# Reordering the opening of a small vision-transformer kernel: TensorE matmuls on constants first, mask coefficients summed on GpSimd

## What is computed

```python
patches = im.reshape(b, c, hp, P, wp, P)                  # P = 8: 256 patches of 2048 numbers per image
x = jnp.einsum('bchpwq,dcpq->bhwd', patches, conv_w)      # 2048 x 128 weights, "conv" below
x = x.reshape(b, hp * wp, -1) + conv_b
for i in range(2):                                        # L = 2 layers, 8 heads of 64
    y = _ln(x, ln1_g[i], ln1_b[i])
    q, k, v = jnp.split(y @ qkv_w[i], 3, axis=-1)
    ...                                                   # softmax(q), softmax(k), ctx = k^T v, att = q ctx
    x = x + att @ out_w[i] + out_b[i]
    x = x + gelu(_ln(x) @ ff1_w[i] + ff1_b[i]) @ ff2_w[i] + ff2_b[i]
h = _ln(x, lnf_g, lnf_b) @ head_w + head_b
h = h + attention3(layernorm(h))
# feed-forward with masks: for e in (96, 144, 192), r in (2, 3, 4): a = alpha_e[e] * alpha_r[r]
C0 = C0 + a * (m_out[:, None] * m_in[None, :])            # m_in = (d < e), m_out = (h < r * e)
h = h + new_gelu(layernorm(h) @ (w_fc * C0).T + b_fc * c0b) @ (w_proj * C1).T + b_proj * c1b
```

## Time and profile before

| | us |
|---|---|
| three timed runs | 151.07, 151.41, 154.46 |
| median of the runs | 151.41 |
| span of the profiled execution (first to last instruction) | 154.1 |
| the run that fits that span, and what it leaves around it | 154.46, 0.4 |
| PE busy / DVE busy / ACT busy / POOL busy within the span | 131.1 / 93.7 / 66.0 / 49.1 |

### The profile page before, as it was taken

The page is one execution under the profiler, slowest core; times in us unless marked ns, Lnnn a source line. Parts: engine busy times, 40 slices in busy tenths (PEclk is TensorE's granted clock), DMA queues, the critical chain, the costliest instruction groups (busy, mean ns, idle before and its releaser), DMA issues.

```text
span 154.1 us, 2173 instructions
## 1 busy us (share of the span) xinstructions
PE 131.1 (85%) x790; PEld 113.1 (73%) x790; DVE 93.7 (61%) x236; ACT 66.0 (43%) x149; POOL 49.1 (32%) x60
## 2 busy tenths in 40 slices
PE   1699889999779989799797996769987959999993
PEld 1468668797658968589576984559876948999992
DVE  1200087947799668977689757773957796145201
ACT  3010313906559746697375981144222040163230
POOL 0000020074162953447553673180671060004000
PEclk9999999999999999999999999956977995599999
DMA  5999997008800000000000000000000000000101
GB/s 161 285 421 415 421 412 262 0 4 265 209 0 0 6 0 0 0 0 4 0 0 0 0 4 0 0 0 2 2 0 0 4 0 0 0 4 0 51 0 51
DMA packets 3388, 11.50 MB, mean 75 GB/s; under 512 B 393, under 2 KB 1385, under 8 KB 3122
## 3 DMA queue, kind: packets, MB, share of 16 engines
q1 hardware_dynamic: 3378, 11.37, 20.6%
HBM read 10.98 MB, written 0.39 MB: 74 GB/s over the span
## 4 chain that ended last, share of the span: by engine, by line
PE 55%; DVE 26%; issue 5%; POOL 5%; ACT 3%; DMA 3%; SPq 0%; DVEq 0%; ACTq 0%; POOLq 0%
PE bank L302 16%; DVE xn L655 10%; PE bank L320 10%; PE bank L437 5%; PE bank L389 5%; PE bank L561 5%; POOL rstd L1103 3%; DMA embed_sb<-in_embed 3%; DVE stats L645 2%; DVE yT_hi L662 2%; DVE nkmax L695 2%; POOL yT_lo L1109 1%; PE bank L336 1%; PE bank L531 1%; PE bank L339 1%
## 5 line engine op out<-in xcount | busy, mean ns | idle before, releaser
L1103 POOL TENSOR_TENSOR rstd<-var,minus_half 128x2 f32<-128x2 f32 x14 | 10.2, 726 | 69.8 <-DVE var L650 69.8
L655 DVE TENSOR_SCALAR xn<-x,mv,rstd 128x128 f32<-128x128 f32 x20 | 13.8, 732 | 4.2 <-POOL rstd L1103 4.2
L320 PE MATMUL bank<-embed_sb 128*128 128x256 f32 x32 | 12.0, 544 | 4.4 <-DMA embed_sb<-in_embed 4.4
L955 ACT ACTIVATE yT<-bank,small_sb 128x256 f32<-128x256 f32 x10 | 5.7, 565 | 19.5 <-DVE yT_hi L662 16.4
L320 PEld LDWEIGHTS bank<-embed_sb 128*128 128x128 f32 x32 | 8.5, 277 | 7.2 <-DMA embed_sb<-in_embed 5.1
L1122 POOL TENSOR_TENSOR qn<-q,rqsum 128x512 f32<-128x512 f32 x8 | 8.2, 1044 | 15.2 <-DVE rqsum L719 15.2
L336 PE MATMUL bank<-small_sb,xn 128*128 128x128 f32 x20 | 4.4, 301 | 7.6 <-DVE xn L655 7.6
L413 PE MATMUL bank<-cw,qT 128*128 128x128 f32 x64 | 10.0, 289 | 0.4
L413 PEld LDWEIGHTS bank<-cw,qT 128*128 128x128 f32 x64 | 8.2, 190 | 2.0 <-issue 1.3
L336 PEld LDWEIGHTS bank<-small_sb,xn 128*128 128x128 f32 x20 | 2.0, 141 | 10.3 <-DVE xn L655 10.3
L975 ACT ACTIVATE kexp<-bank,nkmax 128x256 f32<-128x256 f32 x16 | 7.4, 473 | 4.3 <-DVE nkmax L695 4.3
(11 more groups left out here) (142 smaller groups left out, 349.1 us busy)
## 6 DMA issues: line engine op xcount, KB each, us to landing
embed_sb<-in_embed SPq DMA_DIRECT2D x3, 768.0 KB, 7.9
patches_sb<-in_patches SPq DMA_DIRECT2D x2, 1024.0 KB, 12.1
restw<-in_rest_w SPq DMA_DIRECT2D x2, 768.0 KB, 16.1
qkvw<-in_qkv_w SPq DMA_DIRECT2D x3, 256.0 KB, 11.0
embed_sb<-in_qkv_w SPq DMA_DIRECT2D x1, 768.0 KB, 4.7
embed_sb<-in_embed SPq DMA_DIRECT2D x1, 576.0 KB, 4.4
projw_raw<-in_proj_w SPq DMA_DIRECT2D x1, 576.0 KB, 16.2
embed_sb<-in_fc_w SPq DMA_DIRECT2D x1, 576.0 KB, 7.6
```

The lines of the kernel that those rows point to most:

```text
L320: mm = nc.tensor.matmul(dst[:, 0:TOKENS], embed_sb[:, c, 0:D], rhs, start=(c == 0), stop=(c == KCONV - 1))
L655: last = nc.vector.tensor_scalar(xn[i][:, t, 0:width], src[:, t, 0:width], mv[i][:, t, 0:1], rstd[i][:, t:t + 1], ALU.subtract, ALU.mult)
L1103: nc.gpsimd.tensor_tensor(rstd[i][:], var[i][:], minus_half[:], ALU.pow).then_inc(rstd_ready[i], 1)
```

## The change

1. TensorE's first work is five matmuls of the constant tile `ones` (128x128 by 192 columns) into a bank nobody reads (`warm_up`). They wait only for the first memset of DVE. The first image's 16 chunks then run without the mask matmuls between them.
2. The mask coefficients are no longer made by matmuls. A table of 128 x 9 x 66 numbers (`mix`, 0/1 patterns laid out as the coefficients are used) is loaded with the six alphas, and POOL makes the nine products, weighs the table and adds its nine slices up (`mix_coefficients`, at the end of step 0, behind `ff1w_lo`). DVE's four weighing instructions, PE's nine small matmuls and ACT's three copies are gone.
3. SP's order: the old 9-partition mask load between the second and third piece of the first image is gone; the small constants come one piece later; the second image's patches come in three pieces (chunks 0 to 3, 4 to 7, 8 to 15), the first two where the first half was; the weights of layer 1 come ahead of the projection's; the new table, 297 KB, and the alphas follow them.

```diff
+SECOND_AT = (0, 4, 8, KCONV)
+SECOND_PIECES = len(SECOND_AT) - 1
+WARM_UP = 5
+FC_MIX, PROJ_MIX, BIAS_MIX = 0, ECH * HSEG, ECH * HSEG + HC * (ESEG + 1)
+NMIX = BIAS_MIX + ESEG
...
-        mix_sb = sb("mix_sb", [MIX, HMAX + E + HSEG + ESEG + 2])
+        mix_sb = sb("mix_sb", [P, MIX, NMIX])
+        alphas_sb = sb("alphas_sb", [P, len(EMBED) + len(RATIO)])
...
         @block.sync
         def _(sp):
-            half = KCONV // 2
             for j in range(CONV_PIECES):
                 at = slice(CONV_AT[j], CONV_AT[j + 1])
                 sp.dma_start(embed_sb[:, at, :], embed0[:, at, :]).then_inc(loaded[f"embed{j}"], 16)
-                if j == 1:
-                    sp.dma_start(mix_sb[:], mix).then_inc(loaded["mix"], 16)
+                if j == 2:
                     sp.dma_start(small_sb[:], small).then_inc(loaded["small"], 16)
-            sp.dma_start(patches1_sb[:, 0:half, :], patches1[:, 0:half, :]).then_inc(loaded["patches1a"], 16)
+            def second(j):
+                at = slice(SECOND_AT[j], SECOND_AT[j + 1])
+                sp.dma_start(patches1_sb[:, at, :], patches1[:, at, :]).then_inc(loaded[f"second{j}"], 16)
+            second(0)
+            second(1)
...
-            sp.dma_start(patches1_sb[:, half:, :], patches1[:, half:, :]).then_inc(loaded["patches1b"], 16)
+            second(2)
             sp.dma_start(restw[0][:], rest_w[0]).then_inc(loaded["rest0"], 16)
             sp.dma_start(rows_sb[:], rows.to_broadcast([P, NROW])).then_inc(loaded["rows"], 16)
+            sp.dma_start(restw[1][:], rest_w[1]).then_inc(loaded["rest1"], 16)
+            sp.dma_start(alphas_sb[:], alphas.to_broadcast([P, len(EMBED) + len(RATIO)])).then_inc(loaded["mix"], 16)
+            sp.dma_start(mix_sb[:], mix).then_inc(loaded["mix"], 16)
+            sp.dma_start(headw[:], head_w).then_inc(loaded["head"], 16)
             sp.dma_start(projw_raw[:], proj_w).then_inc(loaded["proj"], 16)
-            sp.dma_start(restw[1][:], rest_w[1]).then_inc(loaded["rest1"], 16)
-            sp.dma_start(headw[:], head_w).then_inc(loaded["head"], 16)
...
+            def warm_up(dst):
+                pe.wait_ge(consts_set, 1)
+                for _ in range(WARM_UP):
+                    nc.tensor.matmul(dst[:, 0:E], ones[:, 0:P], ones[:], start=True, stop=True)
...
-            conv(0, KB[0], 0, CONV_AT[2])
-            mix_fc_masks()
-            conv(0, KB[0], CONV_AT[2], KCONV)
+            warm_up(CB)
+            conv(0, KB[0], 0, KCONV)
             pe.wait_ge(loaded["small"], 16)
             embedding_to_tokens(0, KB[1])
-            pe.wait_ge(mix_copied, 2)
             conv(1, SB_, 0, 6)
...
             head(0)
-            mix_proj_masks()
...
+            def mix_coefficients():
+                pool.wait_ge(loaded["mix"], 32)
+                e, r = alphas_sb[:, 0:len(EMBED)], alphas_sb[:, len(EMBED):]
+                shape = [P, len(EMBED), len(RATIO)]
+                nc.gpsimd.tensor_tensor(alpha[:].rearrange("p (i j) -> p i j", i=len(EMBED)),
+                                        e.unsqueeze(2).to_broadcast(shape), r.unsqueeze(1).to_broadcast(shape),
+                                        ALU.mult).then_inc(mixing, 1)
+                pool.wait_ge(mixing, 1)
+                nc.gpsimd.tensor_tensor(weighted[:], mix_sb[:], alpha[:].unsqueeze(2).to_broadcast([P, MIX, NMIX]),
+                                        ALU.mult).then_inc(mixing, 1)
+                for m in range(1, MIX):
+                    pool.wait_ge(mixing, m + 1)
+                    nc.gpsimd.tensor_tensor(coef[:], weighted[:, 0, :] if m == 1 else coef[:], weighted[:, m, :],
+                                            ALU.add).then_inc(mixing, 1)
+                pool.wait_ge(mixing, MIX + 1)
...
                 if s == 0:
                     weight_low_part("ff1_0", 1, ff1w_all(0), ff1w_parts[0][0][:], ff1w_parts[0][1][:])
+                    mix_coefficients()
```

More of the change, by code:

```diff
@@ L68, with build @@
 CONV_PIECES = len(CONV_AT) - 1
-def build(nc, small, embed0, patches1, qkv_w, rest_w, rows, mix, fc_w, proj_w, head_w, aqkv_w, aout_w, out):
+SECOND_AT = (0, 4, 8, KCONV)
[3 more added lines that the diff above has]
+NMIX = BIAS_MIX + ESEG
+def build(nc, small, embed0, patches1, qkv_w, rest_w, rows, mix, alphas, fc_w, proj_w, head_w, aqkv_w, aout_w, out):
     with ExitStack() as ctx:
@@ L201, in build @@
         loaded = {n: sem(f"loaded_{n}") for n in (
-            ["small", "mix", "rows", "fc", "proj", "head", "aqkv", "aout", "patches1a", "patches1b", "qkv0_k"]
-            + [f"embed{j}" for j in range(CONV_PIECES)]
+            ["small", "mix", "rows", "fc", "proj", "head", "aqkv", "aout", "qkv0_k"]
+            + [f"embed{j}" for j in range(CONV_PIECES)] + [f"second{j}" for j in range(SECOND_PIECES)]
             + [f"qkv{l}" for l in range(LAYERS)] + [f"rest{l}" for l in range(LAYERS)])}
         consts_set = sem("consts_set")
-        alpha_ready = sem("alpha_ready")
-        mix_psum = sem("mix_psum")
-        mix_copied = sem("mix_copied")
+        mixing = sem("mixing")
         split_hi, split_lo = ({n: sem(f"{n}_{part}") for n in ("qkv0", "qkv1", "ff1_0", "ff1_1", "aqkv", "fc")}
@@ L316, in conv @@
                         pe.wait_ge(loaded[f"embed{CONV_AT.index(c)}"], 16)
-                    if i == 1 and c % (KCONV // 2) == 0:
-                        pe.wait_ge(loaded["patches1a" if c == 0 else "patches1b"], 16)
+                    if i == 1 and c in SECOND_AT:
+                        pe.wait_ge(loaded[f"second{SECOND_AT.index(c)}"], 16)
                     rhs = embed_sb[:, c, D:] if i == 0 else patches1_sb[:, c, :]
@@ L439, in ff2 @@
                 mm.then_inc(ff2_done[i], 1)
-            def mix_fc_masks():
-                pe.wait_ge(loaded["mix"], 16)
-                pe.wait_ge(alpha_ready, 3)
-                for c in range(ECH):
-                    nc.tensor.matmul(SB_[0:EC, c * HSEG:(c + 1) * HSEG], alpha_mask_e[:, c * EC:(c + 1) * EC],
-                                     mask_hseg, start=True, stop=True)
-                nc.tensor.matmul(SB_[:, 128:128 + E], alpha[:], mask_e, start=True, stop=True).then_inc(mix_psum, 1)
-            def mix_proj_masks():
-                for c in range(HC):
-                    at = c * (ESEG + 1)
-                    mm = nc.tensor.matmul(KB[1][:, at:at + ESEG + 1], mask_h[:, c * P:(c + 1) * P], alpha_eseg[:],
-                                          start=True, stop=True)
-                mm.then_inc(mix_psum, 1)
+            def warm_up(dst):
+                pe.wait_ge(consts_set, 1)
+                for _ in range(WARM_UP):
+                    nc.tensor.matmul(dst[:, 0:E], ones[:, 0:P], ones[:], start=True, stop=True)
             def head(i):
@@ L1254 @@
     mask_e = np.array([[u < e for u in range(E)] for e in EMBED for r in RATIO], np.float32)
-    alpha_e = np.repeat(a["L0_ffn_alpha_e"], len(RATIO))[:, None]
-    alpha_r = np.tile(a["L0_ffn_alpha_r"], len(EMBED))[:, None]
+    masks = np.zeros((P, MIX, NMIX), np.float32)
+    in_e = mask_e.reshape(MIX, ECH, EC).transpose(2, 0, 1)
+    masks[:EC, :, FC_MIX:PROJ_MIX] = (in_e[:, :, :, None] * mask_h[None, :, None, ::SEG]).reshape(EC, MIX, -1)
+    in_h = mask_h.reshape(MIX, HC, P).transpose(2, 0, 1)
+    seg_e = np.concatenate([mask_e[:, ::SEG], np.ones((MIX, 1), np.float32)], axis=1)
+    masks[:, :, PROJ_MIX:BIAS_MIX] = (in_h[:, :, :, None] * seg_e[None, :, None, :]).reshape(P, MIX, -1)
+    masks[:, :, BIAS_MIX:] = mask_e[None, :, ::SEG]
+    alphas = np.concatenate([a["L0_ffn_alpha_e"], a["L0_ffn_alpha_r"]])[None]
     host = {
@@ L1259 @@
         "qkv_w": a[T + "qkv_w"], "rest_w": np.stack(rest), "rows": rows,
-        "mix": np.concatenate([mask_h, mask_e, mask_h[:, ::SEG], mask_e[:, ::SEG], alpha_e, alpha_r], axis=1),
+        "mix": masks, "alphas": alphas,
         "fc_w": _chunks(a["L0_ffn_w_fc"].T, EC), "proj_w": _chunks(a["L0_ffn_w_proj"].T, P),
```

37 lines of the change are left out of this document (9 added, 28 removed).

## The result

| | runs | median us | lowest to highest |
|---|---|---|---|
| before, beside it | 4 | 152.94 | 151.07 to 155.28 |
| after | 4 | 153.57 | 153.40 to 153.86 |
| before, second series | 24 | 154.73 | 149.50 to 156.41 |
| after, second series (e5) | 12 | 153.72 | 150.95 to 157.30 |

The ratio after to before was 1.0156 (1.0122 to 1.0191) in the first series and 1.0052 (0.9977 to 1.0127) in the second. The ratios leave out runs more than 1.5% above the fastest of their kernel, and in the first series those are two of the four runs of before (154.46 and 155.28). Over all runs the median rose by 0.6 us in the first series and fell by 1.0 in the second, where the mean rose by 0.5: no change that can be told from none. I had forecast 148.9 with a range up to 151.9.

What follows compares the result with a forecast made beforehand. The prediction took a chain of hand-overs between engines as the bound, PE's clock and masks setting the first embedding's end. Terms -4.0 (opening) and +1.5 (POOL) gave -2.5 us, 151.4 to 148.9, range 146.7 to 151.9.

Steps and rivals of the forecast that it cites:

- opening: warm-up, masks, loads: First image's embedding: it would end at 13.9 instead of 17.9 us, a gain of 4.0 us (3.4 to 4.4).
- Warm-up and loads: Opening: full clock from 8.2 us, chunks then paced by loads, the fifth piece landing at 12.0, embedding ending at 13.9.
- What the warm-up replaces: Before's opening: PE at 1.2 GHz until 14.9 us, embedding ending at 17.9; difference to the new end, 4.0 us, counted as gain.
- DVE's and ACT's mask instructions stood in idle time (0): Opening: removing the mask instructions of DVE and ACT was claimed to gain nothing, 0 us.
- Second image's pieces ahead of the qkv weights: Loads: splitting the second image's patches would cost 0.4 us of SP time and nothing on the path.
- POOL's ten instructions: POOL ahead of step 1's rstd: mixing takes 5.1 us, making the second xn 1.5 us late (0.2 to 2.7).
- Mixing hidden: Rival, step 1: POOL's mixing delays xn by 0.2 us or less; -4.0 us, 147.4; chance 20%.
- the clock rises no sooner: Rival, opening: clock still rises at 14.9, embedding ends at 16.8, gain only 1.1; 151.8 us; chance 15%.
- The clock falls back: Rival: PE's waits for loads and in step 1 invite one more half-clock spell, costing 2.8; 151.7 us; chance 13%.
- The lower end of the range: Whole kernel: 146.7 us, with the load at its best and the delay from POOL gone.
- POOL's upper bound: POOL's ten mixing instructions: 6.3 us in all, taking 0.18 us for each wait.

Runs made afterwards that it cites:

- e5: The changed kernel, unchanged, run 12 more times; 153.72 us median, ratio to before 1.0052.
- e13: The kernel before with filler matmuls on constants in PE's waits, with more of them around the projection's masks; 150.61 us median.
- e14: The changed kernel with ScalarE's table loaded early, POOL's mixing moved to step 0's idle time, and fillers in the steps and last part; 147.31 us median.
- e16: The changed kernel with filler matmuls in PE's waits and nothing else changed, same kernel as e10; 149.69 us median.
- e10: The changed kernel with filler matmuls in PE's waits and nothing else changed; 149.46 us median, ratio to before 0.9698.
- e9: The kernel before with filler matmuls in the steps and last part, none where its projection masks stand; 149.43 us median, ratio to before 0.9667.
- e2: The changed kernel with one small ScalarE copy at the very start, so its activation table loads early; 152.85 us median, ratio to before 1.0145.
- e4: The changed kernel with ScalarE's table loaded early and POOL's mixing moved to step 0's idle time, no fillers; 152.35 us median, ratio to before 1.0148.
- e8: e4 with filler matmuls on constants in PE's waits, in the last part and the four steps; 146.59 us median, ratio to before 0.9701.
- e12: e4 with six 5-column matmuls on constants behind the head, where before's mask matmuls stood; 151.10 us median, ratio to before 0.9778.
- e7: e4 with 20 filler matmuls of 128 columns in PE's waits behind the head; 146.83 us median, ratio to before 0.9719.

## Why the prediction was wrong, step by step

The forecast of -2.5 us had two terms; the means of the last series and of the second show four:

| term | forecast | measured |
|---|---|---|
| opening: warm-up, masks, loads | -4.0 | -1.9, an estimate (-3.0 from e13 to e14, less the 1.1 of e13's own fillers) |
| ScalarE's table load | 0 | +1.0 to +1.85 |
| POOL's mixing | +1.5 | +1.2 |
| net with fillers | -2.5 | -0.8 (e16 less e13), +0.3 without the 1.1 |
| more time at half clock | 0 | +1.7, an estimate |
| sum | -2.5 | +2.0 by the terms, +0.5 measured |

The first three terms are steps in a row from e13 to e16, so that they add up to the net by construction; that is no check of them. The net has a standard error of 0.7, and e10 less e9, the same pair on another chip, is -0.2. What was measured without fillers is e5's mean of 154.14 (standard error 0.64) less that of before beside it, 153.65 (0.44). The estimate for the clock: e5's runs rise from 150.95 at 10.1 us of half clock to 157.30 at 30.8, 0.31 for each us, and after had 5.4 more of them than before (19.1 against 13.7, standard error 2.1). The two sums are 1.5 apart, with standard errors of about 1.0 and 0.8, so the account is no closer than that.

*Warm-up and loads: right in their mechanism.* Pace, waits and the new bound (loads) came as said, with 14.4 for 13.9. But the piece that bounds is the fourth and not the fifth: the last wait is 0.26 at 10.51, and 16 records took 3.88 behind it.

*What the warm-up replaces: mis-sized, -1.9 for -4.0.* "Before ... was up by 14.9" was true of the one profile. Profiles of the same opening show 14.9, 14.5, 9.2 and 7.5, and the embedding ending between 15.2 and 17.9. The gain over the latest of them was carried to a median of all. I even wrote that the runs before differ by 3.4 us, and laid all of it on the late spells.

*"DVE's and ACT's mask instructions stood in idle time (0)": the step that failed.* It put at nothing a term of 1.0 to 1.85 us. The copies were worth nothing as work, but ahead of the first of them the table load stood at 0.73. With them gone the load moved behind the wait for the embedding, onto the chain. The Trainium skill has the rule that would have warned me, in "ScalarE: Activation LUTs", "Step-by-step: what each stage is for": the load is placed right before the ACTIVATE that needs the set. The traces agree: at 0.73 ahead of a copy in e2, at 14.47 ahead of `embT` in after, 1.28 us both times. What they leave open is why before's load stood ahead of the wait of its copy, which ran at 10.19, while after's stood behind the wait of `embT`; in the program one wait precedes that copy and two precede `embT`.

*Second image's pieces ahead of the qkv weights: right.* `qkvw_hi` waited 0.20 us, and ACT finished at 18.1; nothing on the chain waited for it.

*POOL's ten instructions: right, 1.2 for 1.5.* POOL's timeline in after:

```profile
36.59 0.21 POOL L1114 TENSOR_TENSOR alpha<-alphas_sb 128x9 f32<-128x9 f32 x1
36.88 1.18 POOL L1118 TENSOR_TENSOR weighted<-mix_sb,alpha 128x594 f32<-128x594 f32 x1
38.14 0.30 POOL L1122 TENSOR_TENSOR coef<-weighted 128x66 f32<-128x66 f32 x1
38.52 2.81 POOL L1122 TENSOR_TENSOR coef<-coef,weighted 128x66 f32<-128x66 f32 x7
41.41 0.70 POOL L1080 TENSOR_TENSOR rstd<-var,minus_half 128x2 f32<-128x2 f32 x1
```

From 36.59 to 41.3 it is 4.7 us for 5.1 forecast, 0.07 for each wait for its own result. `xn` waited 0.67 us for `rstd` and ended with `qkvw_lo` (44.12 and 44.02): the lock that the Trainium skill describes in "SBUF — State Buffer", "Who interferes with whom", showed again.

*The rivals.* "Mixing hidden" and "the clock rises no sooner" are out. "The clock falls back" is what happened, with 13% far too low, and it is the second term that the sum had at nothing: by the estimate above as large as the table load, but the less certain of the two. It named the cause, PE's longer wait in step 1 (2.27 us, and a fall 1.4 us behind it), but other executions fell elsewhere: e5 shows no fall there and 10.2 us from 96.5. The amount is what can be told, not the place. Its price of 2.8 for a spell of 6.9 us was too high: the spell of 3.4 us cost 0.9, and at 0.31 for each us 6.9 us cost 2.1. The rule of the Trainium skill in "TensorE: Matmul & The Clock Gate", "What's actually happening", that the ramp is worth under 1% of a typical span, is not what these runs show: with the rise at 14.9 instead of 9.2 the same embedding ended 2.7 us later, 1.8% of 150 us. The later falls are worth more: 5.9 between the means of e4 (152.52) and e8 (146.66), which ran on two chips.

*The sums.* The lower end of the range should have been 147.0 (151.4 - 4.4), not 146.7, and POOL's upper bound 6.1, not 6.3; neither decides anything.

What remains open: why after had more half clock than before. The removed mask matmuls behind the head are a candidate, which e12 left undecided; the longer waits in the first 45 us are another. Its size is uncertain too: the mean of before was 12.8 to 16.0 us by chip.

## What to carry to other kernels

Before an instruction is deleted as free, ask what it triggered: here the load of ScalarE's table stood ahead of the first activation, and went with it; a dummy activation at the start buys that back. When runs of one kernel differ by some per cent, put the mean granted clock of each run beside its time before reading one profile as the kernel, and size a clock term over several executions. Where PE waits for other engines again and again, try a few matmuls on constants in the waits first (e7, e8): only then could changes of 1 us be measured here. Look in the trace that the engine still waits behind them; e13's did not, and cost 1.1 us.

## What the runs showed of the hardware that was not expected

One and the same opening has its first clock rise anywhere from 7.5 to 14.9 us, and the unchanged kernel before spends 3.5 to 17.5 us at half clock (3.5, 10.7, 13.7 and 17.2 come again and again); its time follows, 149.5 to 156.4. After had up to 30.8 us. Twenty filler matmuls of 128 columns in the last part (e7) took the later falls away: 0 us in five of six runs, where the same kernel without them (e4) had 17 to 21. The granted-clock column reads 1.00 ahead of the first rise though the records run at half pace: the earlier trace rows has 436 ns for a record beside 1.00, and 214 behind the rise.
